# VectorE copies each tile's W2 into one of four buffers two tiles ahead, TensorE holds no registers; ScalarE copies W1 of tile 0 behind the gelu table

## What is computed

```python
x = x + tanh(g_xattn) * attention(layernorm(x), ctx, ctx)      # softmax over the 64 keys of a sequence
h = layernorm(x)
route = sigmoid(h @ Wr + br)                                    # 8 experts, the best one is taken
for e in range(8):
    y = gelu(h @ W1[e]) @ W2[e]                                 # 128 -> 512 -> 128
    out += (argmax(route) == e) * y
x = x + tanh(g_ffn) * out * max(route)
```

## Time and profile before

| | before |
|---|---|
| median of 3 runs | 137.18 us (136.96 to 137.32) |
| span of the profiled execution | 133.2 us, 4155 instructions |
| what lies around the span, against the median | 4.0 us |
| TensorE busy | 124.1 us (93%) |
| VectorE busy | 82.4 us (62%) |
| ScalarE busy | 92.9 us (70%) |
| GpSimd busy | 96.1 us (72%) |

### The profile page before, as it was taken

How to read it: one execution, slowest core, us unless ns; L and a number is a source line. 1 busy time by engine, 2 the same in 40 slices (tenths; PEclk the granted TensorE clock), 3 DMA queues, 4 the chain that set the end, 5 groups by cost and what they waited for, 6 DMA issues and landing times.

```text
span 133.2 us, 4155 instructions
## 1 busy us (share of the span) xinstructions
PE 124.1 (93%) x1201; PEld 109.3 (82%) x1201; DVE 82.4 (62%) x520; ACT 92.9 (70%) x215; POOL 96.1 (72%) x144
## 2 busy tenths in 40 slices
PE   5989999999999895999999999999999999999970
PEld 2659677778578562999999999999999999999970
DVE  2799998799998999797566368331432332233230
ACT  0658598685995488887698687759684986878310
POOL 7548979678778687877678557787777877745544
PEclk9999999999999999999999999999999999999999
DMA  3989999994011216152411532256441111110000
GB/s 107 236 204 283 304 359 335 287 285 112 20 46 41 65 25 162 41 122 68 102 48 60 143 102 66 81 139 175 108 123 42 50 40 40 59 44 22 16 5 0
DMA packets 20096, 15.20 MB, mean 114 GB/s; under 512 B 6622, under 2 KB 16994, under 8 KB 20074
## 3 DMA queue, kind: packets, MB, share of 16 engines
q1 hardware_dynamic: 17570, 10.62, 30.7%
q0 software_dynamic: 2272, 4.27, 9.6%
q10 hardware_dynamic: 232, 0.04, 0.1%
HBM read 10.12 MB, written 5.26 MB: 115 GB/s over the span
## 4 chain that ended last, share of the span: by engine, by line
PE 57%; POOL 7%; DMA 5%; issue 4%; SPq 0%; ACT 0%; DVE 0%; POOLq 0%
PE banks_o L1353 26%; PE banks_v L1344 13%; PE bank_q L1344 7%; PE bank_p L1344 6%; POOL scratch L432 5%; PE bank_x L1336 3%; DMA scratch<-rows,row_at 3%; DMA tok<-scratch 2%; POOL rows L428 2%; POOL out_dram L447 1%; ACT tokn L550 0%; SPq L336 0%; DVE tok L949 0%; PE bank_s L1442 0%; PE bank_s L1315 0%
## 5 line engine op out<-in xcount | busy, mean ns | idle before, releaser
L1353 PE MATMUL banks_o<-w_sb,hT 128*128 x312 | 41.8, 277 | 0.2
L432 POOL DMA_INDIRECT scratch<-rows,row_at x32 | 31.4, 982 | 12.9 <-issue 6.9
L1353 PEld LDWEIGHTS banks_o<-w_sb,hT 128*128 128x128 f32 x312 | 38.0, 192 | 0.8 <-issue 0.5
L949 DVE SCALAR_TENSOR_TENSOR tok<-banks_o,tok 128x128 f32<-128x128 f32 x39 | 13.7, 350 | 38.9 <-PE banks_o L1353 37.2
L447 POOL DMA_INDIRECT out_dram<-tok x21 | 20.7, 986 | 6.4 <-issue 5.2
L447 POOL DMA_INDIRECT out_dram<-tok,token_at x18 | 17.7, 983 | 9.8 <-DVE tok L949 7.2
L550 ACT ACTIVATE tokn<-tok 128x128 f32<-128x128 f32 x39 | 19.0, 486 | 6.7 <-PE bank_x L1336 3.3
L490 ACT COPY w_now<-w_sb 128x512 f32 x39 | 23.6, 606 | 0.0
L1344 PE MATMUL banks_v<-toknT,w_now 128*128 128x128 f32 x160 | 21.1, 275 | 0.0
L1344 PEld LDWEIGHTS banks_v<-toknT,w_now 128*128 128x128 f32 x160 | 19.4, 192 | 0.0
L556 ACT ACTIVATE hT<-banks_v 128x512 f32<-128x512 f32 x20 | 11.9, 596 | 8.8 <-PE banks_v L1344 8.8
(11 more groups left out here) (178 smaller groups left out, 225.8 us busy)
## 6 DMA issues: line engine op xcount, KB each, us to landing
tok<-scratch SPq DMA_DIRECT2D x39, 66.0 KB, 2.0
w_sb<-in_L_ffn_W_dram SPq DMA_DIRECT2D x1, 2048.0 KB, 11.5
x_all<-in_x_dram SPq DMA_DIRECT2D x7, 256.0 KB, 3.9
ctx<-in_ctx_dram SPq DMA_DIRECT2D x8, 128.0 KB, 3.7
scratch<-pad_rows SPq DMA_DIRECT2D x1, 528.0 KB, 17.5
scratch<-rows,row_at POOLq DMA_INDIRECT x32, 2.7
out_dram<-tok POOLq DMA_INDIRECT x21
out_dram<-tok,token_at POOLq DMA_INDIRECT x18
```

Source lines behind the costliest of these rows:

```text
L432: nc.gpsimd.indirect_dma_start(out=scratch, out_offset=bass.IndirectOffsetOnAxis(ap=row_at[:, g * GT + t:g * GT + t + 1], axis=0), in_=row ...
L949: nc.vector.scalar_tensor_tensor(out=tok[j][:, 0:D], in0=y_ps[j % 2], scalar=tok[j][:, SCALE:TOKEN], in1=tok[j][:, 0:D], op0=ALU.mult, op1 ...
L1353: last = nc.tensor.matmul(y_ps[j % 2], hT[j % DEEP][:, c * P:(c + 1) * P], w2_sb[:, bass.ds(w_at[j] + c * D, D)], start=(c == 0), stop=(c ...
```

## The change

TensorE's register loads go, with all its registers; `down` reads W2 from one of four buffers `w2_now`. VectorE gets the register loads and a copy of 128x512 per tile: `copy_w2(0)` and `copy_w2(1)` ahead of its loop, then `copy_w2(j + 2)` behind `copy_transposed(j + 3)`. `down(j)` waits for the copy. On ScalarE, `experts_of(0)` and `copy_w1(0)` stand ahead of `normalise_tile(0)`.

```diff
+        w2_now = [sb(f"w2_now_{i}", [P, F]) for i in range(DEEP)]
...
             def normalise_tile(j):
-                if j in BATCH_AT:
+                if j > 0 and j in BATCH_AT:
                     experts_of(BATCH_AT[j])
...
             nc.scalar.activation(gelu_table[:], tanh_gates[:], ACT.Gelu)
+            experts_of(0)
             act.wait_ge(expert_w_in, 16 * 2)
+            copy_w1(0)
             normalise_tile(0)
-            copy_w1(0)
...
+            w_regs = [dve.alloc_register(f"wv{m}") for m in range(RING)]
+            w_at = {}
+
+            def experts_of(i):
+                stage, first, n = BATCHES[i]
+                dve.wait_ge(table_ready, stage + 1)
+                dve.reg_load(w_regs[0:n], weights_at[0:1, first:first + n])
+                for u, r in enumerate(w_regs[0:n]):
+                    w_at[first + u] = dve.snap(r, min_val=0, max_val=(E - 1) * F)
+
+            def copy_w2(j):
+                if j < FFN_TILES:
+                    if j in BATCH_AT:
+                        experts_of(BATCH_AT[j])
+                    after(dve, y_done, j - DEEP)
+                    nc.vector.tensor_copy(w2_now[j % DEEP][:], w2_sb[:, bass.ds(w_at[j], F)]).then_inc(w2_copied, 1)
...
             cap_ends(1)
+            dve.wait_ge(expert_w_in, 16 * 2)
+            copy_w2(0)
+            copy_w2(1)
             for j in range(FFN_TILES):
                 residual2(j)
                 copy_transposed(j + 3)
+                copy_w2(j + 2)
...
             def down(j):
                 pe.wait_ge(gelu_done, j + 1)
+                pe.wait_ge(w2_copied, j + 1)
                 after(pe, y_added, j - 2)
                 for c in range(FC):
                     last = nc.tensor.matmul(y_ps[j % 2], hT[j % DEEP][:, c * P:(c + 1) * P],
-                                            w2_sb[:, bass.ds(w_at[j] + c * D, D)], start=(c == 0), stop=(c == FC - 1))
+                                            w2_now[j % DEEP][:, c * D:(c + 1) * D], start=(c == 0), stop=(c == FC - 1))
...
-            experts_of(0)
-            pe.wait_ge(expert_w_in, 16 * 2)
             pe.wait_ge(place_done, NG - 4)
...
             for j in range(FFN_TILES):
-                if j in BATCH_MIDDLE and BATCH_MIDDLE[j] + 1 < len(BATCHES):
-                    experts_of(BATCH_MIDDLE[j] + 1)
                 down(j)
```

More of the change, by code:

```diff
@@ L55, in attention_moe @@
     BATCH_AT = {first: i for i, (_, first, _) in enumerate(BATCHES)}
-    BATCH_MIDDLE = {first + n // 2: i for i, (_, first, n) in enumerate(BATCHES)}
     LAST_STAGE = len(STAGES) - 1
@@ L266, in attention_moe @@
         toknT_done, h_done, y_done = sem("toknT_done"), sem("h_done"), sem("y_done")
-        gelu_done, w1_copied = sem("gelu_done"), sem("w1_copied")
+        gelu_done, w1_copied, w2_copied = sem("gelu_done"), sem("w1_copied"), sem("w2_copied")
         def live(g):
@@ L1320, in prefix @@
                                  start=False, stop=True).then_inc(prefix_done, 1)
[L1322 to L1330, removed]
             def transpose_tile(j):
```

## The result

| | before | changed |
|---|---|---|
| median, first comparison (4 runs each) | 137.07 us (135.84 to 137.32) | 139.37 us (138.34 to 142.47) |
| ratio | | 1.0205 [1.0143, 1.0266] |
| median, second comparison, another chip (17 and 6 runs) | 136.28 us (135.07 to 137.42) | 140.82 us (139.47 to 141.75) |
| ratio | | 1.0309 [1.0244, 1.0375] |

What follows compares the result with a forecast made beforehand. TensorE's gapless tile loop was taken as the bound. Span 133.2 + 3.1 (late first copies) − 1.13 (TensorE's loads) + 0.25 (VectorE's loop work) = 135.4, with 4.0 around it 139.4 us, 1.6% slower; range 138.0 to 143.8.

Steps and rivals of the forecast that it cites:

- TensorE's loads, −1.13: TensorE's tile loop: seven register loads go; their excess at tiles 2, 19, 24 and 30 saves 1.13 us.
- The late first copies, +3.1: Head of the tile loop: `down(0)` waits for VectorE's first W2 copy behind `cap_ends(1)`, delaying everything after by 3.1 us.
- The clock at its level throughout: Expected profile sign: TensorE's granted clock stays at its upper level, 2.4 GHz, for the whole changed kernel.
- Rival C: TensorE's standstill near 55 us lowers the clock; one tile at half speed costs 1.9 us, total 141.3; chance 0.08.
- VectorE's work in the loop, +0.25: VectorE's added copies and loads exceed the slack in iterations 11 to 13, where it makes long tables: 0.25 us.
- around tile 16: Expected profile sign: one small TensorE stall there, the only exception to `down` without "issue" or length over 0.9 us.
- just fits, cost 0: Group 6, placed in iteration 4, returns as tile 13: VectorE 0.84 us later against 0.88 to spare, so no cost.
- The base: Profiled execution of before: span 133.2 us plus 4.0 us around it, making the median of 137.18.
- A: VectorE bounds the first 14 tiles, each W2 copy taking 0.69 us: total 141.1 us; chance 0.20.
- B: VectorE's copies hold up GpSimd's indirect DMAs, which set the end from 0.08 us per instruction; 144.6 us at 0.24; chance 0.15.
- D: `down(0)` isn't held, as VectorE has both copies done by 54.98; only −1.13 remains: 136.05 us; chance 0.07.
- ScalarE, 0: Ahead of the loop: W1 copy starts `tokn` of tile 0 0.2 us later, covered by tile 1's rows; cost 0.

Runs made afterwards that it cites:

- e9: Kernel before plus VectorE's load and first two W2 copies, awaited by `down(0)` and `down(1)`, with twelve filler products on TensorE: 138.56 us, ratio 1.0152 to before.
- e10: Changed kernel, but TensorE reads W2 of tiles 0 to 4 in place and VectorE copies from tile 5 on: 135.24 us, ratio 0.9944 to before.
- e8: The changed kernel, unaltered, run again beside the kernel before: 140.82 us, ratio 1.0309 to before.
- third set: Runs of e8, e9 and e10 on one chip beside the unchanged kernel before, which takes 136.28 us there.
- e4: Kernel before with ScalarE's part alone, W1 copy of tile 0 ahead of its normalisation: 170.95 us against 170.47, ratio 1.016 to before.

## Why the prediction was right, and where it wasn't

**TensorE's loads, −1.13: right.** Of it 0.83 belongs to tiles 19, 24 and 30. From tile 17 to 38 before took 40.13 and the changed kernel 39.23, −0.9, and every profile without these loads gave 39.23 to 39.37, every one with them 39.95 to 40.36. The 0.30 of tile 2 can't be read apart in the changed kernel. In e9, which keeps that load, tiles 1 to 17 took 30.85 instead of 31.15: behind a late start it cost nothing, so at least part of the 0.30 would have gone without the change too.

**The late first copies, +3.1: right in mechanism and as a wait, too large as time.** The prediction's chain from `scale_logits` to `down(0)` was 57.95 − 55.96 = 1.99 us; in the profile it is 58.73 − 56.71 = 2.02. From the start of `cap_ends(1)` to that of the copy it is 0.85 (0.87 by the prediction), and a copy takes 0.418 instead of 0.48. TensorE's idle time was 2.96 and 3.13 us, against 2.97 by the prediction's own numbers. The starting point of that chain was off: the one profile of before has VectorE released by GpSimd's `rstd2` at 55.96, these have 56.71 and 56.74, and e9 and e10, which change less, have 56.53 and 56.45. In time e9 puts the term at 2.1 us (by its ratio), a third less than predicted, with the loads still in. The excess of tile 2's load is hidden there (0.3); the rest of the difference isn't accounted for.

**"The clock at its level throughout": wrong. This is the step that failed.** Rival C had a chance of 0.08, and it occurred in the profiled execution of each comparison (mean clock 0.971 and 0.975). Three more of the second comparison have 0.974 or 0.975 and, by that, most likely the same fall; one of the first (0.984) and two of the second (0.982, 0.986) may have it in part, but before itself has such means; the other two of the first (0.995 and 0.997) kept the clock. The evidence given against it was only that gaps were shorter before and the clock never fell. That says nothing of a gap of 3 us, and the sum itself produced that gap. C's price was 1.9 us (one tile at the lower level) for a total of 141.3; it is 2.6 us in e8, since one and a half tiles run at half speed.

**VectorE's work in the loop, +0.25: right in place, short in size.** In the second comparison's profile tiles 1 to 17 are 0.2 longer; with the 0.30 of tile 2 given back that is 0.5. The predicted stall "around tile 16" is there, in TensorE's timeline of that profile, from the transpose of tile 16 to that of tile 17:

```profile
87.68 0.28 PE L1348 MATMUL bank_x<-ident,tokn 128*128 128x128 f32 x1
...
89.84 0.30 PE L1348 MATMUL bank_x<-ident,tokn 128*128 128x128 f32 x1
```

This is 2.16 us, where an undisturbed tile takes 1.90, and the next step takes 1.99: 0.35 in all against 0.25. Tiles 1 to 17 of e10 give 0.95 by the same reckoning, in the first comparison's profile 2.1, of which 1.12 is the stall of tile 13, the place that "just fits, cost 0". It did fit in the second comparison, by 0.21 us (0.04 by the prediction). But with the slack used up, an execution in which the DMAs take 1.4 us longer pays most of it, and the prediction gave that no price.

**The base.** The prediction took 4.0 us around the span, from a median and one profile of different executions. Every later run lists both, and what lies around the span is 1.8 as a rule (142.47 and 140.7, 140.92 and 139.1; 1.78 in the median of before's 17 executions in the third set). With that the profiled execution of before took an estimated 135.0, and before's spans in the third set reach from 133.3 to 135.4. So some 2.2 of the 4.0 were time that an ordinary execution of before loses inside its span. This made up for what the sum lacked: the predicted span was 135.4, the measured ones are 136.6 and 136.8 at a mean clock of 0.995 and 0.997, and 137.7 to 140.7 in the eight executions at 0.971 to 0.986. That the number 139.4 is the median of the first four is luck: errors of opposite sign cancelled, and a set with one more fallen clock would have had a higher one. The predicted ratio of 1.016 lies within the first interval and below the second.

**A** fell: the copy takes 0.418 us, not 0.69. At 512 columns this is under the 1.07 ns a column of the earlier trace rows. The VectorE page of the Trainium skill, "VectorE: DVE Perf Modes", section on Mode 2×_2P, has a float32 copy within SBUF at two elements per cycle, and the trace agrees in kind: 0.14 us longer than the 0.281 of a 128-column copy out of PSUM.

**B** fell by its size. GpSimd's scatters into `scratch` take 1003 ns in the mean (982 before), those into `out_dram` 1001 and 983 (986 and 983 before), so 0.02 or less per instruction, against the 0.08 from which B decides. Single ones that meet a copy are longer, in the timeline of GpSimd, first comparison:

```profile
58.22 1.19 POOL L432 DMA_INDIRECT scratch<-rows,row_at  x1 [0.30 <-issue]
...
72.84 1.31 POOL L432 DMA_INDIRECT scratch<-rows,row_at  x1 [4.09 <-DVE row_at L703]
74.45 0.96 POOL L432 DMA_INDIRECT scratch<-rows,row_at  x1 [0.30 <-issue]
```

Those at 58.22 and 72.84 lie over copies at 58.15 and 72.83. The same instructions took 0.96 and 1.03 in the profile of before. In the first comparison's profile 29 of GpSimd's DMA instructions overlap a copy of VectorE; 24 of them take 0.96 to 1.00, as without a copy, and five take 1.13 to 1.31, where only one of before's 71 is over 1.04. The Trainium skill, page "SBUF — State Buffer", section "SBUF: two separate sides", says that GpSimd can't write the descriptors of its DMAs while VectorE runs such a copy. This trace agrees only in part: at most some 0.3 us on a meeting, and nothing on most.

**D** did not occur: `down(0)` was held in both profiles of the change. e10 is what D would have given, and D's −1.1 was near: −0.8 by the ratio.

**ScalarE, 0:** not refuted. e8 has ScalarE's new order and e9 the old, and `down(0)` waits for VectorE in both; e10 has the new one, does `up(0)` at 52.84 (52.77 before) and is faster than before. In the changed kernel's two profiles `up(0)` is at 53.28 and 53.23, half a microsecond later than before. The gelu table ahead of the new order is already 0.8 us later in them, so the new order isn't shown to be the cause, and the wait for the first copy hides the delay. e4 alone was unclear.

**Left open:** what the changed kernel takes with fillers on an undisturbed chip; why it was faster than before with them on the disturbed ones (by 1.0 to 2.7%); why two of its first four executions kept the clock and four or more of the six on the second chip did not; why executions of before differ by 2 us inside the span; and the 170 us chips.

## What to carry to other kernels

When a sum yields a new idle gap on TensorE, price what follows the gap as well as the gap: here 3 us of waiting cost 2.6 more at half speed, and twelve products on dummy data removed that part. Moving a small cost off the critical engine (1.1 us over seven places) pays only if the first use of the moved result isn't late; reading the first tiles in place turned a loss of 3.1% into a gain of 0.6%. And a span of one execution should not be joined to the median of others: take the difference from runs that list both.

## What the runs showed of the hardware that was not expected

- TensorE's clock was granted at 0.50 for some 5.5 us (58.8 to 64.3) behind an idle gap of 3.0 to 3.1 us, and had already sunk within the gap (0.83 in the mean of the stretch from 55 to 58.8). The same gap filled with products left it at 1.00. Of the same program's executions some had the fall and some, going by the mean clock, had not.
- A copy of 128x512 float32 within SBUF takes VectorE 0.418 us, less than twice that of 128 columns out of PSUM, 0.281.
- A register load of four to six entries takes VectorE 0.85 to 1.54 us, of which 0.55 (e9) to 1.23 stood as idle time ahead of the next copy where it was seen.
- Rows written by the same scatters, begun within 0.05 us of the same time, came back 1.4 us apart in two executions of the changed kernel.
- On three chips one and the same program took 25% longer than on two others, with common pauses of TensorE, VectorE and ScalarE of up to 7.4 us.
